# Tile 1 projected chunk by chunk beside tile 0, context loads held back, 128 extra matmuls at the start

## The reference, cut to what matters

```python
q = jnp.einsum('bse,edh->bsdh', x, Wq) + bq
k = jnp.einsum('bse,edh->bsdh', x, Wk) + bk
v = jnp.einsum('bse,edh->bsdh', x, Wv) + bv
k = jnp.repeat(k, SCALE, axis=-1)
v = jnp.repeat(v, SCALE, axis=-1)
scores = jnp.einsum('bsdh,bseh->bsde', q, k) / np.float32(np.sqrt(D))
attn = jax.nn.softmax(scores, axis=-1)
out = jnp.einsum('bsde,bseh->bsdh', attn, v)
...
x = _layernorm(x + attention(x))
x = _layernorm(x + matmul(fake_quant(x), fake_quant(ctx)))
x = _layernorm(x + ffn(x))
```

## Time and profile before

| | |
|---|---|
| median of 3 runs | 630.72 us (629.39 to 633.28) |
| the profiled execution | 629.14 us |
| its span, first to last instruction | 627.3 us |
| PE busy | 593.6 us (95% of the span) |
| DVE, ACT, POOL busy | 382.1, 299.1, 123.9 us |
| mean granted clock of PE | 0.992 |

### The profile page before, as it was taken

How to read it: one execution, slowest core, us unless ns; L and a number is a source line. 1 busy time by engine, 2 the same in 40 slices (tenths; PEclk the granted TensorE clock), 3 DMA queues, 4 the chain that set the end, 5 groups by cost and what they waited for, 6 DMA issues and landing times.

```text
span 627.3 us, 9388 instructions
## 1 busy us (share of the span) xinstructions
PE 593.6 (95%) x3728; PEld 476.8 (76%) x3728; DVE 382.1 (61%) x515; ACT 299.1 (48%) x384; POOL 123.9 (20%) x162
## 2 busy tenths in 40 slices
PE   2799999998999899999999999999999999999993
PEld 1687877666776688788888888888888888888882
DVE  4947898889854355335333331338864565749976
ACT  4556688896684544333333342114344333323824
POOL 2811355735442022422210000000000000021000
PEclk9999999998999999999999999999999999999998
DMA  9766675673663668779998774203433336089913
GB/s 335 286 186 187 183 203 167 170 259 106 194 203 135 241 239 317 263 274 344 315 344 314 252 253 121 77 1 101 135 91 86 94 99 235 1 275 328 293 55 124
DMA packets 82252, 123.61 MB, mean 197 GB/s; under 512 B 23840, under 2 KB 50720, under 8 KB 82208
## 3 DMA queue, kind: packets, MB, share of 16 engines
q1 hardware_dynamic: 74592, 94.95, 45.6%
q0 software_dynamic: 5168, 19.40, 9.3%
q10 hardware_dynamic: 2448, 8.65, 4.3%
HBM read 83.13 MB, written 35.65 MB: 189 GB/s over the span
## 4 chain that ended last, share of the span: by engine, by line
PE 65%; DVE 1%; ACT 0%; issue 0%; ACTq 0%
PE psum L1552 33%; PE psum L1611 30%; PE psum L1519 0%; PE psum L1528 0%; PE psum L1527 0%; PE psum L1545 0%; DVE ffn_lo L1959 0%; DVE ffn_lo L1948 0%; ACT hx L1714 0%; ACT ffn_lo L1724 0%; DVE stat_n L1940 0%; DVE ffn_lo L1933 0%; DVE x1T_lo L1809 0%; PE psum L1536 0%; ACT x1T_hi L1645 0%
## 5 line engine op out<-in xcount | busy, mean ns | idle before, releaser
L1813 DVE TENSOR_TENSOR u_lo<-u_raw,u_hi 128x1024 fp32r<-128x1024 f32 x18 | 24.7, 1373 | 73.7 <-ACT u_hi L1650 73.7
L1552 PE MATMUL psum<-x1T_hi,u_hi 128*128 128x512 f32 x160 | 62.9, 393 | 0.7 <-DVE x1T_lo L1809 0.7
L1552 PE MATMUL psum<-x1T_hi,u_lo 128*128 128x512 f32 x160 | 62.3, 389 | 0.0
L1552 PE MATMUL psum<-x1T_lo,u_hi 128*128 128x512 f32 x160 | 62.3, 389 | 0.0
L1611 PE MATMUL psum<-x2T_lo,x2T_hi 128*128 128x512 f32 x264 | 62.1, 389 | 0.0
L1611 PEld LDWEIGHTS psum<-x2T_lo,x2T_hi 128*128 128x128 f32 x264 | 49.6, 188 | 10.3
L1552 PE MATMUL psum<-x2T_hi,u_hi 128*128 128x512 f32 x144 | 56.5, 392 | 0.0
L1552 PE MATMUL psum<-x2T_lo,u_hi 128*128 128x512 f32 x144 | 56.1, 389 | 0.0
L1552 PE MATMUL psum<-x2T_hi,u_lo 128*128 128x512 f32 x144 | 56.0, 389 | 0.0
L2090 POOL DMA_DIRECT2D x1T_hi<-r_scratch x4 | 2.9, 713 | 243.9 <-PE psum L1611 243.9
L1611 PE MATMUL psum<-x1T_hi,x2T_hi 128*128 128x512 f32 x216 | 50.4, 389 | 0.0
(11 more groups left out here) (258 smaller groups left out, 1237.3 us busy)
## 6 DMA issues: line engine op xcount, KB each, us to landing
d_raw<-in_L_ffn_down_w_dram SPq DMA_DIRECT2D x20, 512.0 KB, 7.7
t_scratch<-d_raw SPq DMA_DIRECT2D x20, 512.0 KB, 5.1
d_raw<-t_scratch SPq DMA_DIRECT2D x20, 512.0 KB, 3.8
c_sb<-in_ctx_dram ACTq DMA_DIRECT2D x16, 512.0 KB, 3.9
u_raw<-in_L_ffn_up_w_dram SPq DMA_DIRECT2D x16, 512.0 KB, 5.2
r_scratch<-f1b SPq DMA_DIRECT2D x10, 512.0 KB, 4.4
r_scratch<-f2b SPq DMA_DIRECT2D x10, 512.0 KB, 3.1
x_sb<-in_x_dram SPq DMA_DIRECT2D x8, 512.0 KB, 5.8
```

Of the source, the lines that this page charges most:

```text
L1552: mm = pe.matmul(acc_b[:, product_index(m, b) % 4], s, v, start=(k == 0 and i == 0), stop=(k == KT - 1 and i == 2))
L1813: dve.tensor_tensor(u_lo[:, m % 2], u_raw[:, m % 2], u_hi[:, m % 2].bitcast(F32), ALU.subtract).then_inc(S["u_lo_done"], 1)
```

## The change

PE's list now starts with 18 matmuls of the bf16 identity on itself (`warm`), the transposes of tile 0, 110 more such matmuls and the transposes of tile 1. Then come the chunks of tiles 0 and 1 together (`project_early`). Tile 1 adds up in the PSUM pair of the context product (`xa_ps`), so `column_sums(0)` waits until `qkv_out(1)` has emptied it. The rows of tile 1 are loaded behind chunk 3 of the weights. The first two context loads wait until the last chunk of the weights is there. `transpose_x(2)` moves ahead of the last chunk of tile 1, and `project(2, 0)` ahead of `scores(0)`. All five lists are written in another order to the end of the first part.

```diff
+        qkv_of = lambda t: xa_ps if t == 1 else qkv_ps
...
             for k in range(KT):
                 load_w(k)
-            load_x(1)
+                if k == 3:
+                    load_x(1)
...
+            def project_early(t, k):
+                if k == 0:
+                    pe.wait_ge(S["xT_lo_done"], t + 1)
+                pe.wait_ge(S["wq_lo_done"], k + 1)
+                pe.wait_ge(S["wkv_lo_done"], k + 1)
+                mm = contract(t, k)
+                if k == KT - 1:
+                    mm.then_inc(S["qkv_ready"], 1)
...
             def project(t, part):
                 if part == 0:
                     pe.wait_ge(S["xT_lo_done"], t + 1)
-                    if t >= 1:
-                        pe.wait_ge(S["qkv_evac"], t)
+                    pe.wait_ge(S["qkv_evac"], 1 if t == 2 else t)
...
+            def warm(n):
+
+                pe.wait_ge(S["masks_done"], 3)
+                for _ in range(n):
+                    pe.matmul(sc_ps[:, 0:TQ].rearrange("p n d -> p (n d)"), so["ident_bf"][:], so["ident_bf"][:], start=True, stop=True)
...
             def column_sums(b):
                 pe.wait_ge(S["c_done"], (b + 1) * CK)
+                if b == 0:
+                    pe.wait_ge(S["qkv_evac"], 2)
...
+            warm(18)
             transpose_x(0)
-            project(0, 0)
+            warm(110)
             transpose_x(1)
-            project(0, 1)
-            project(1, 0)
-            project(1, 1)
+            project_early(0, 0)
+            project_early(1, 0)
+            project_early(0, 1)
+            project_early(1, 1)
+            project_early(0, 2)
+            project_early(1, 2)
+            project_early(0, 3)
+            project_early(1, 3)
+            project_early(1, 4)
+            project_early(0, 4)
+            project_early(0, 5)
+            project_early(0, 6)
+            project_early(1, 5)
+            project_early(0, 7)
+            project_early(1, 6)
             transpose_x(2)
+            project_early(1, 7)
+            project(2, 0)
             scores(0)
-            project(2, 0)
+            project(2, 1)
             values(0)
-            project(2, 1)
             transpose_x(3)
...
             def load_context(c):
                 if c >= 2:
                     act.wait_ge(S["c_done"], c - 1)
+                if c < 2:
+                    act.wait_ge(wraw_in[KT - 1], 48)
                 act.dma_start(c_sb[:, c % 2], c_tiles[c]).then_inc(c_in[c % 2], 16)
...
             split_w(3)
+            xT_hi_out(1)
             split_w(4)
+            load_context(0)
             split_w(5)
-            load_context(0)
             split_w(6)
             split_w(7)
-            xT_hi_out(1)
             load_context(1)
```

More of the change, by code:

```diff
@@ L326, in transpose_x, with contract @@
                 mm.then_inc(S["xT_ready"], 1)
+            def contract(t, k):
+                st = [x[:, t % 2, k] for x in (xT_hi, xT_lo)]
+                for i in range(3):
+                    for c0, c1 in ((0, BANK), (BANK, QKV)):
+                        s, v = split_products(st, [w[:, k, c0:c1] for w in (w_hi, w_lo)])[i]
+                        mm = pe.matmul(qkv_of(t)[:, c0:c1], s, v, start=(k == 0 and i == 0), stop=(k == KT - 1 and i == 2))
+                return mm
+            def project_early(t, k):
[6 more added lines that the diff above has]
+                    mm.then_inc(S["qkv_ready"], 1)
             def project(t, part):
@@ L480, in _ @@
             project(4, 0)
+            column_sums(0)
+            values(2)
             project(4, 1)
-            values(2)
+            transpose_x(5)
+            transpose_q1(0)
             scores(3)
-            transpose_x(5)
-            column_sums(0)
+            cross(0)
             project(5, 0)
-            transpose_q1(0)
             values(3)
             project(5, 1)
+            transpose_q1(1)
             transpose_x(6)
-            cross(0)
             scores(4)
-            transpose_q1(1)
+            cross(1)
             project(6, 0)
             project(6, 1)
-            cross(1)
+            transpose_q1(2)
             values(4)
             scores(5)
-            transpose_q1(2)
             transpose_x(7)
@@ L502, in _ @@
             project(7, 0)
+            scores(6)
             transpose_q1(3)
-            scores(6)
             project(7, 1)
@@ L509, in _ @@
             transpose_expert(1)
+            values(6)
             column_sums(1)
-            values(6)
+            transpose_q1(4)
             transpose_expert(2)
             transpose_expert(3)
-            transpose_q1(4)
+            cross(4)
             scores(7)
-            cross(4)
+            transpose_x2(0)
             w2_product(0)
             w2_product(1)
-            transpose_x2(0)
             w2_product(2)
+            values(7)
             transpose_x2(1)
-            values(7)
             w2_product(3)
@@ L985, in _ @@
             prepare(2)
+            prepare(3)
             prepare_lo(1)
-            prepare(3)
+            prepare_lo(2)
+            prepare_lo(3)
+            xT_lo_out(1)
             prepare(4)
-            prepare_lo(2)
             prepare(5)
             prepare(6)
-            prepare_lo(3)
             prepare(7)
+            quant_constants()
             prepare_lo(4)
@@ L1072, in _ @@
             first_stats(4)
-            ctx_magic(15)
             softmax_max(6)
```

300 lines of the change are left out of this document (146 added, 154 removed).

## The result

| kernel | median, us | ratio to before, 95% interval |
|---|---|---|
| before | 630.99 (629.39 to 633.28) | |
| after | 639.37 (637.75 to 640.77) | 1.0138 [1.0108, 1.0168] |

The change makes the kernel slower by 1.4%, 8.4 us between the medians. The forecast was 634.4 us.

A forecast was written before the change was run, and what follows sets the result against it. PE, busy 95% of the span, bounds the kernel, with nearly all that can be won in the first 53 us. +5.2 at scores(1) less 1.5 recovered gave +3.7 us: 632.8 profiled, 634.4 on the median; range 627.0 to 639.5.

The forecast's parts named there:

- The front's term: Start up to scores(1): scores(1) at 58.7 us against 53.48, so +5.2 us.
- the term for the rest: Behind scores(1): a quarter of 6.2 us of waits recovered, -1.5 us.
- The parameters: Four tiny loads that quant_constants waits for on DVE: expected at 28.5 or 27.1 us, taken as 28.0.
- DVE's wait: DVE idle before the first of quant_constants, released by a DMA, 3 to 5 us.
- PE's idle: PE without work ahead of chunk 4, from 25.1 to 29.3 us: 4.2 us.
- The four subtractions: DVE's weight splits that PE needs from chunk 4 on, behind quant_constants: 0.6 us taken for one.
- the small instructions ahead: DVE's small instructions between the parameters' landing and chunk 4's subtraction: 0.7 us.
- PE's idle ahead of scores(0): PE waits from 45.9 us for tile 0's regrouping and key blocks, ready at 48.2: 2.3 us.
- From there to the end: From scores(1) on: 6.2 us of waits could go, a quarter taken as recovered, 1.5 us.
- Rival 4: Steps moved ahead on PE meet inputs 5 us late; one stall, no recovery: +8.7 us, 639.4; 17%.
- Rival 1: Parameters land early, DVE isn't held, tile 1 ends 5.9 us ahead: -2.2 us, 628.5; 12%.
- Rivals 2 and 3: 2: the new order later takes all waits, 629.7, 12%. 3: the front's gain passes whole, 623.3, 9%.

The follow-up runs named there:

- new_front_old_rest: The changed kernel's lists up to scores(1) on every engine, those of the kernel before from there on; 636.93 us, ratio 1.0102.
- old_late_part: The changed kernel's lists up to transpose_expert(1), those of the kernel before behind it; 637.45 us, ratio 1.0110.
- late_untangled: The changed kernel with residual(5) behind fc2_lo_out(3) on DVE and transpose_x2(0) behind w2_product(1) on PE; 638.41 us, ratio 1.0109.
- tile0_first: The changed start with tile 0's chunks ahead of tile 1's and the parameters behind all splits, before's lists from scores(1) on; 631.84 us, ratio 1.0017.
- the four corners: The changed kernel with quant_constants early or late, new or old lists from scores(1): 639.37 (early, new), 635.02 (late, new), 636.93 (early, old), 632.34 us (late, old).
- quant_late: The changed kernel with quant_constants moved on DVE from ahead of prepare_lo(4) to behind prepare_lo(7); 635.02 us, ratio 1.0079.
- pool_yields: tile0_first with one wait more: from chunk 5 on, POOL splits a chunk only when DVE has split the chunk before; 630.22 us, ratio 1.0010.
- t2_early: pool_yields with tile 2's transposes between tile 0's last chunk and tile 1's last three, their copies as early; 631.38 us, ratio 1.0024.

## Why the prediction was right and where it failed

The sum gave +3.7 us and +8.4 were measured. The front's term missed by 0.3 us in the trace, the term for the rest by some 4.

**The front: right, nearly line by line.** The parameters were put at 28.0 us and stood ready at 28.2; DVE's wait was forecast at 3 to 5 us and was 4.05; PE's idle at 4.2 and was 4.63; tile 0's projection at 37.3 for 38.5; scores(0) at 48.2 for 48.16; values(0) at 55.4 for 55.08; `transpose_x(3)` at 57.7 for 57.33; scores(1) at 58.7 for 58.94, +5.46 against the +5.2 of the sum. The two edits of `quant_constants` show the cause: 3.7 us in the changed kernel, 4.2 in the other. The drop of the clock behind chunk 4's wait came, with 4.63 us of idle; the Trainium skill ("TensorE: Matmul & The Clock Gate", HAM oscillation) had it as due, and the trace agrees with the page here. That the times agree to within 0.3 us is luck in part. Four kernels have the same lists up to scores(1) (after, new_front_old_rest, old_late_part, late_untangled), and their traces have scores(0) at 48.16 to 49.76 and scores(1) at 58.94 to 59.92: +5.5 to +6.4.

Inside it, errors that cancelled. The four subtractions took 0.37 us each and not 0.6; the small instructions ahead took 1.8 us and not 0.7, since one of them stood until POOL ended; the held context load was priced as a rival on the queue only, and the 2.43 us that it holds ACT's splits weren't seen. Tile 0's projection ended 1.2 us later than forecast, and its regrouping took 8.6 us up to the key blocks (38.52 to 47.13) where 9.7 were taken. PE's idle ahead of scores(0), put at 2.3 us, was 0.87, and the lower clock in the transposes of tile 3, 0.6 us, wasn't forecast. The bytes ahead of the parameters are 7.3 MB, not 6.8: two tiles of rows and the weights. With neither the parameters nor that hold in the way (tile0_first), POOL's back-to-back splits held chunk 4 to 28.77 all the same.

**"From there to the end": the failed step.** The sum took a quarter of 6.2 us as recovered, -1.5. In the traces the stretch from scores(1) to the second part grew from 154.25 to 160.25 us; between the medians it is 8.4 less the 5.5 to 6.4 of the front, +2 to +3 us. The reason given, that the context steps are less late and leave DVE and ACT freer, named no wait that would go. Nearly nothing of the waits went: the 1.79 us of the earlier trace rows is still there with 1.57, at 152.48. Only the lower clock behind it went (64 products in 1.95 us at 157.89, where before took 3.56), 1.6 us. More than that came. New lists against old ones cost 1.6 to 2.3 us (the four corners). The one large new wait is the stall at 162 us, 2.25 and 1.01 us and 1.4 for the lower clock behind it; how much of the lists' price it carries isn't settled, since late_untangled, which took out the first of the two, gained 1.0 to 1.8 us within the intervals. The lower clock after `transpose_x(3)` stretched the products of scores(1) to 2.95 us from 1.95, 0.5 of which before had as a wait, in this execution. And the old rest behind the new front doesn't recover 1.5 us either: it takes 153.9 to 157.3 us in six traces, against 154.25.

**Rival 4** (slower by more, 639.4) had the size, and its kind: one more stall with its drop of the clock and no recovery. It had the wrong place: `column_sums(0)`, `transpose_q1(0)` and `cross(0)` weren't what stalled, and the condition, inputs 5 us late, was wrong as well, since quant_late stalls with 1.5 us. What stalls was set by two orders. PE's has `transpose_x2(0)` ahead of `w2_product(0)` and `(1)`, so that PE reaches the x2 reload 2.6 us after its issue and not 9.3; putting it back took that wait away (late_untangled). SP's has `load_fc2(3)` and `load_residual(5)` behind `ungroup(5)`, which holds `fc2_lo_out(3)`. The diffs of both lists showed it and the prediction passed over it. **Rival 1** (parameters early) fell with the landing at 28.2; its own sum, though, that an early end of tile 1 wins little because tile 0's attention sets scores(1), is what pool_yields and t2_early show. Where DVE isn't held (quant_late), its scores(0) at 42.3 and scores(1) at 52.8 came 2.5 and 2.1 us later, partly by the biases and `ctx_magic(0)` ahead of `qkv_out(0)`. **Rivals 2 and 3** fell.

Not settled: the 0.53% that remain with the old rest and the late parameters. Part may be the order of tile 0's chunks, the held context load and `ctx_magic(0)` ahead of `qkv_out(0)`, since tile0_first, which changes all of these, has 0.17%, with an interval that just overlaps; the runs don't part them. The two corners that give the new rest's price overlap in their intervals; that it costs something rests on both pairs and on the traces together. Each kernel has one trace, so a difference of a us between two traces is no more than a hint.

## What to carry to other kernels

A step that waits for a small, late DMA costs its whole wait to everything behind it in its engine's list, so before moving it, look up the landing and not the size. Where lists are fitted to each other, a reordering later on is a cost until a named wait is shown to go; look at the diff for two things, a consumer that is put ahead of work that hid its load (`transpose_x2(0)` here), and, in the DMA queue's list, what now stands behind a long row of issues. When a start is made faster, the next producer (here tile 2's split rows, then the key blocks) takes over within a few us.
